# A two-layer transformer kernel: the last batch's tail reordered, second-layer heads one to a slot

## What is computed

```python
x = L0_attn_query
xn = _layernorm(x, axis=-1)
x = x + _L0_attn_ref(xn, ...) + _L0_ffn_ref(xn, ...)
xn = _layernorm(x, axis=-1)
x = x + _L1_attn_ref(xn, ...) + _L1_ffn_ref(xn, ...)
```

## Time and profile before

| | |
|---|---|
| median of 3 runs | 957.77 us (956.62 to 958.67) |
| the profiled execution | 958.63 us, span 956.8 us |
| TensorE (matmuls) busy | 830.6 us, 87% |
| VectorE busy | 742.3 us, 78% |
| ScalarE busy | 689.1 us, 72% |
| GpSimd busy | 471.4 us, 49% |
| TensorE clock granted, mean | 0.937 of full |

### The profile page before, as it was taken

The page is one execution under the profiler, slowest core; times in us unless marked ns, Lnnn a source line. Parts: engine busy times, 40 slices in busy tenths (PEclk is TensorE's granted clock), DMA queues, the critical chain, the costliest instruction groups (busy, mean ns, idle before and its releaser), DMA issues.

```text
span 956.8 us, 21194 instructions
## 1 busy us (share of the span) xinstructions
PE 830.6 (87%) x7120; PEld 609.9 (64%) x7120; DVE 742.3 (78%) x2028; ACT 689.1 (72%) x1973; POOL 471.4 (49%) x734
## 2 busy tenths in 40 slices
PE   3555538999899999999999999999999999996763
PEld 1123225687677777777777777777777777764541
DVE  6988855766768788887878787878787878875684
ACT  2654625656669778887888888788778878884673
POOL 1443332412326565665666555656565656566452
PEclk9675778999999999999999999999999999998896
DMA  9543412212243456554564555455556554544454
GB/s 331 196 148 110 133 52 82 52 34 43 48 103 75 90 93 140 102 83 108 123 105 78 115 116 111 77 124 102 107 80 143 89 101 89 123 98 93 114 107 102
DMA packets 283179, 100.97 MB, mean 106 GB/s; under 512 B 241344, under 2 KB 281024, under 8 KB 281920
## 3 DMA queue, kind: packets, MB, share of 16 engines
q1 hardware_dynamic: 280368, 97.27, 45.9%
q10 hardware_dynamic: 2704, 2.36, 0.7%
HBM read 30.38 MB, written 10.49 MB: 43 GB/s over the span
## 4 chain that ended last, share of the span: by engine, by line
PE 68%; DVE 9%; ACT 3%; issue 2%; DMA 1%; POOL 1%; SPq 0%; POOLq 0%; DVEq 0%; ACTq 0%
PE ps L666 42%; PE ps L716 9%; PE ps L816 4%; PE ps L799 4%; PE ps L692 3%; DVE arena L660 2%; PE ps L825 2%; PE ps L801 2%; PE ps L729 2%; DVE arena L999 1%; ACT arena L655 1%; DMA arena<-arena 1%; ACT arena L875 1%; DVE arena L659 1%; DVE nb L1006 1%
## 5 line engine op out<-in xcount | busy, mean ns | idle before, releaser
L660 DVE SCALAR_TENSOR_TENSOR arena<-ps,bqk,arena 128x256 bf16<-128x256 f32 x416 | 187.4, 479 | 63.3 <-ACT arena L655 61.8
L666 PE MATMUL ps<-arena,wqkv 128*128 128x256 bf16 x1728 | 215.2, 275 | 6.5 <-PEq L210 6.5
L655 ACT ACTIVATE arena<-ps,bqk 128x256 bf16<-128x256 f32 x416 | 177.9, 466 | 30.0 <-PE ps L666 20.8
L666 PEld LDWEIGHTS ps<-arena,wqkv 128*128 128x128 bf16 x1728 | 161.7, 98 | 48.1 <-issue 28.3
L1174 POOL TENSOR_SCALAR arena<-arena,rc 128x128 f32<-128x128 f32 (+1 forms) x256 | 106.3, 428 | 174.4 <-DVE rc L1022 174.4
L875 ACT ACTIVATE arena<-arena,nb 128x128 f32<-128x128 f32 (+1 forms) x256 | 114.3, 447 | 90.0 <-DVE nb L999 89.4
L1165 POOL TENSOR_TENSOR arena<-arena 128x512 bf16<-128x512 f32 x107 | 124.8, 1167 | 69.8 <-ACT arena L654 69.8
L1181 POOL TENSOR_SCALAR arena<-arena,rc 128x256 f32<-128x256 f32 x256 | 120.1, 483 | 75.7 <-DVE rc L1026 75.7
L654 ACT ACTIVATE arena<-arena 128x384 bf16<-128x384 f32 (+1 forms) x256 | 136.6, 572 | 18.7 <-POOL arena L1181 9.8
L875 ACT ACTIVATE arena<-ps,nb 128x256 f32<-128x256 f32 x256 | 118.6, 473 | 13.3 <-DVE nb L1006 10.8
L716 PE MATMUL ps<-wo,arena 128*128 128x256 bf16 x768 | 105.6, 274 | 10.5 <-DVE arena L660 9.8
(11 more groups left out here) (98 smaller groups left out, 1286.4 us busy)
## 6 DMA issues: line engine op xcount, KB each, us to landing
arena<-scratch_qk SPq DMA_DIRECT2D x96, 64.0 KB, 2.2
arena<-arena SPq DMA_TRANSPOSE x256, 2.7
scratch_qk<-arena SPq DMA_DIRECT2D x32, 128.0 KB, 1.9
arena<-in_x SPq DMA_DIRECT2D x4, 512.0 KB, 8.6
arena<-in_w_gating SPq DMA_DIRECT2D x2, 1024.0 KB, 6.7
arena<-in_w_q SPq DMA_DIRECT2D x2, 1024.0 KB, 8.6
scratch_xT<-arena ACTq DMA_DIRECT2D x8, 256.0 KB, 6.4
arena<-in_w_k SPq DMA_DIRECT2D x2, 1024.0 KB, 6.4
```

Of the source, the lines that this page charges most:

```text
L655: return nc.scalar.activation(out, in_, ACT.Identity, bias=bias)
L660: return nc.vector.scalar_tensor_tensor(out=out, in0=in_, scalar=bias, in1=hi, op0=ALU.add, op1=ALU.subtract)
L666: last = nc.tensor.matmul(out, lhsT, rhs, start=(n == 0), stop=(n == len(steps) - 1))
```

## The change

It touches the tables of slots and the order of steps from slot 131 on.

- `LATE` is 106, and the heads from there on have **one slot each**, 134 to 155, where they had two to a slot. The pipeline has ten more slots.
- The low part of these heads **alternates**: even heads on GpSimd, odd heads on VectorE (`low_on_pool`).
- In the last batch `x1_sum`, `variance`, `rstd_1` and `normalise` are in one slot, 131, ahead of that slot's maximum.
- The turn is in slot 132 and q/k/v in slot 133, one sooner. Their high and low parts come first in the slot on ScalarE and VectorE, and the q/k/v products first on TensorE.
- The hidden pieces and the down products are one slot sooner too (from slots 134 and 136), and the first steps of `up_gate` wait for x1T explicitly.

```diff
-        LATE = (B - 1) * H1 - 5
+        LATE = (B - 1) * H1 - 6
...
-            return start1(n // H1) + 12 + n % H1 if n < LATE else start1(LASTB) + 7 + (n - LATE) // 2
+            return start1(n // H1) + 12 + n % H1 if n < LATE else start1(LASTB) + 6 + n - LATE
...
-            return start1(b) + (7 + 2 * m if b < LASTB else 7 + m)
+            return start1(b) + (7 + 2 * m if b < LASTB else 6 + m)
...
-            return start1(b) + (6 if b < LASTB else 5)
+            return start1(b) + (6 if b < LASTB else 4)
...
+        def low_on_pool(n):
+            return n < LATE or n % 2 == 0
...
-        ln_in = by_slot(lambda b: start1(b) + 4, B)
+        ln_in = by_slot(lambda b: start1(b) + (4 if b < LASTB else 3), B)
...
                 upto(pe, v0_lo, min(s // 2 + 1, NG0 // 2))
+                pe.wait_ge(x1T_lo, b + 1)
...
             for s in range(SLOTS):
+                last = s >= NG0
+                if last:
+                    for n in pieces_in[s]:
+                        proj_qkv1(n)
                 if 0 <= s - 1 < NG0:
                     scores0(s - 1)
...
+                last = s >= NG0
+                if last:
+                    for b in turns_in[s]:
+                        x1T_low(b)
+                    for n in pieces_in[s]:
+                        qkv1_low(n)
                 if 0 <= s - 1 < NG0:
                     max_0(s - 1)
                 if 0 <= s - 4 < NG0:
                     o0_low(s - 4)
+                if last:
+                    for b in x1_in[s]:
+                        x1_sum(b)
                 for b in ln_in[s]:
                     variance(b)
+                    if last:
+                        normalise(b)
                 for n in heads_in[s]:
                     max_1(n)
...
                 for n in heads_in[s - 1]:
-                    if n >= LATE:
+                    if not low_on_pool(n):
                         p1_low(n)
```

More of the change, by code:

```diff
@@ L552, in hidden_slot @@
             b, m = divmod(n, KH)
-            return start1(b) + (7 + 2 * m if b < LASTB else 7 + m)
+            return start1(b) + (7 + 2 * m if b < LASTB else 6 + m)
         def down_slot(n):
             b, k = divmod(n, KH)
-            return start1(b) + (16 + k if b < LASTB else 9 + k)
+            return start1(b) + (16 + k if b < LASTB else 8 + k)
         def y_slot(b):
@@ L563, in piece_slot @@
             b, w = divmod(n, 3)
-            return start1(b) + ((7, 8, 11)[w] if b < LASTB else 6)
+            return start1(b) + ((7, 8, 11)[w] if b < LASTB else 5)
         def piece_bank(n):
@@ L645, in p1_split @@
         def p1_split(eng, n):
-            if n < LATE:
-                upto(eng, p1_lo, n + 1)
+            if low_on_pool(n):
+                upto(eng, p1_lo, sum(low_on_pool(z) for z in range(n + 1)))
             else:
-                upto(eng, p1_late, n - LATE + 1)
+                upto(eng, p1_late, sum(not low_on_pool(z) for z in range(n + 1)))
         def high(out, in_, bias=None):
@@ L859, in pe_program @@
                     transpose_x1(b)
-                for n in pieces_in[s]:
-                    proj_qkv1(n)
+                if not last:
+                    for n in pieces_in[s]:
+                        proj_qkv1(n)
                 if 0 <= s - 3 < NG0:
@@ L961, in act_program @@
             for s in range(SLOTS):
+                last = s >= NG0
+                if last:
+                    for b in turns_in[s]:
+                        x1T_high(b)
+                    for n in pieces_in[s]:
+                        qkv1_high(n)
                 if 0 <= s - 4 < NG0:
@@ L1145, in dve_program @@
                     rec_1(n)
-                for b in x1_in[s]:
-                    x1_sum(b)
+                if not last:
+                    for b in x1_in[s]:
+                        x1_sum(b)
                 if v_in(s) is not None:
@@ L1151, in dve_program @@
                     hidden(n)
[L1152 to L1157, removed]
+                if not last:
+                    for b in turns_in[s]:
+                        x1T_low(b)
+                    for n in pieces_in[s]:
+                        qkv1_low(n)
+                    for b in ln_in[s]:
+                        normalise(b)
                 for b in y_in[s]:
```

## The result

| | before | after |
|---|---|---|
| median of the runs | 957.77 us | **974.2 us** (970.64 to 976.07) |
| ratio | | **1.0161**, 95% interval 1.0144 to 1.0179 |
| profiled execution, span | 958.63, 956.8 us | 970.64, 968.8 us |
| VectorE busy, 905 to 935 us | 25.08 of 30 us | 16.82 of 30 us |

The ratio and its interval are those on record; the two medians of the table alone give 1.0172. The change makes the kernel slower, as forecast, but the time was missed: the forecast was 967.8 us for the median and 968.6 for the profiled execution, with a range of 962 to 974, and the median of 974.2 lies 0.2 us above that range. Four more executions of the same kernel (run 1) have a median of 972.87, inside it.

The account below looks back on a forecast made before the run. The prediction took VectorE's work and the engines' hand-offs, shared by two heads, as the bound. Start plus 3.2, heads 106 to 127 plus 7.6, tail minus 0.8 made plus 10.0 us: 967.8 us, range 962 to 974.

Parts of the forecast that it names:

- The ring of the earlier trace: Late heads: exponentials, reciprocal, norm, high part, next exponentials across three engines; some 2.85 us per head alone in a slot.
- The start, +3.2: Up to head 106's exponentials: sooner x1, but q/k/v's parts stand ahead of head 105; head 106 at 888.95, plus 3.2 us.
- Hidden slots, 26.0 us: Slots 134 to 141, one head and a hidden piece each: eight steps at 3.25 us, 26.0 us.
- Bare slots, 38.4 us: Slots 142 to 155, a head alone: 13 steps at 2.85 us plus 0.45 us on each of three, 38.4 us.
- Tail, -0.8: From head 127's exponentials to the end: an output's low part no longer stands ahead of its low part, minus 0.8 us.
- VectorE's work as the bound: Rival: VectorE's work sets the late heads' pace, so moving low parts off it gives 948 us; chance 0.06.
- No difference: Rival: slots are only an order, so the time stays within 0.2%, at 959.8 us; chance 0.05.
- TensorE slow in hidden slots: Rival: TensorE granted only 1.2 GHz from slot 134 on, 7.7 us more, 975.5 us; chance 0.10.
- VectorE and GpSimd in each other's way: Rival: GpSimd's low part meets the hidden piece's cast in four hidden slots, 4.5 us more, 972.3 us; chance 0.09.
- Low parts at nothing: Late heads: alternating low parts between GpSimd and VectorE isn't on the way to the next head, so costs nothing.

Follow-up runs that it names:

- Run 8: Run 7's kernel with VectorE's low parts of the bare slots one slot later, ahead of the reciprocal; 964.01 us, ratio 1.0061.
- run 5: The changed kernel with all low parts of the late heads on VectorE, still one head to a slot; 973.22 us, ratio 1.0164.
- run 10: The changed kernel with two heads to a slot, q's reads in slot 135, k's in 136, and all low parts on VectorE; 955.83 us, ratio 0.9976.
- Run 4: The changed kernel with SyncE's twelve reads of q and k spread three to a slot over slots 135 to 138; 968.0 us, ratio 1.0116.
- Run 6: The changed kernel with the attention products of the bare slots two slots later; 972.69 us, ratio 1.0157.
- run 2: The kernel before with only one edit, heads from LATE on one to a slot; 971.14 us, ratio 1.0141.
- Run 7: Run 6's kernel with, in bare slots, ScalarE's high part of the previous head behind the next head's exponentials, low parts moved back too; 967.66 us, ratio 1.0103.

## Why the prediction was right on the bound and missed the time

**The bound.** Right. The ring of the earlier trace rows set the pace of one head to a slot, and VectorE is 56% busy where under 60 was forecast. GpSimd's norm waits for the reciprocal, though not each time as forecast: from 917 to 955 us 9 times, while ScalarE's high part waits for the norm 13 times. Where it doesn't wait, a low part on GpSimd fills the time until the reciprocal is there (918.77 + 1.15 = 919.92, the reciprocal at 919.63 + 0.17). Run 8 shows the ring from the other side. The rule of the Trainium skill ("Perfetto Trace Analysis", Identifying the Most-Contended Engine) to optimise the busiest engine first would have given 948 us with one head to a slot; run 5 shows its step at no change, and run 10 shows the same step at 2.8 us with two heads to a slot, where VectorE is 75 to 80% busy.

**The start, +3.2.** Measured +2.5. The turn started at 875.25 us and q/k/v at 877.60, each 0.9 sooner than forecast, of which 0.74 is the earlier start of the last projection, a matter of chance. Head 105 came at 884.31, where 885.7 was forecast. One term inside was too small: the normalising took 1.56 us where 0.91 was taken, beside GpSimd's low part (last section).

**Hidden slots, 26.0 us.** Seven of eight steps are 3.17 us where 3.25 was taken, 0.6 less together. The eighth is 6.04. **This is the step that failed:** "SyncE issues these reads ahead of the transposes of heads 106 and 107, which has room: a high part asks for the transpose of three heads earlier". It had not. Twelve issues at 0.5 us are 6.0 us of SyncE's queue, and a transpose behind them belongs to an attention product only two slots later. The step was taken at 3.25 us and measured 6.04. The 0.5 us stands in the trace of before, in SyncE's queue:

```profile
893.73 5.74 SPq L1268 DMA_DIRECT2D arena<-scratch_qk  x12
```

I looked at how early the reads came, and not at how long they hold the queue. Run 4 took this wait away and 2.7 us with it.

**Bare slots, 38.4 us.** Measured 39.58, so 0.09 us a step too few. Four heads cost 2.81 + 2.80 + 3.36 + 3.25 = 12.2 us and not 11.85: behind an output two steps are longer, not one. Run 6 got 1.1 us of that back.

**Tail, -0.8.** Measured -0.75, and for the reason given: head 127's low part starts 2.95 us after its exponentials (958.23 and 955.28), where it started 3.69 after.

**Sum.** 2.8 for the reads, 1.2 in bare slots, less 0.7 at the start and 0.6 in hidden slots, are 2.7 us over the forecast in the end (12.7 against 10.0). The profiled execution took 970.64 where 968.6 was forecast; it began the last projection 0.74 us sooner than before. The median lies another 3.6 us higher, where I took it 0.86 below.

So of the 6.4 us between forecast and median, 2.0 stand in the trace and 4.4 in a second step that failed: "The median of the runs, 957.77, lies 0.86 lower". It took one profiled execution of the kernel before as the measure for another kernel, and one execution can't show that. Here the profiled execution was the fastest of four, as it was in runs 1 and 2. What makes the others slower is not shown. Up to 2.7 us can be TensorE's clock in slots 137 and 138, as in the profile of run 6, and 2.2 us lies ahead of the last projection in run 1 (870.21 against 868.00). How often that happens stays open, with two traces of this kernel.

**The rivals.** VectorE's work as the bound: refuted for one head to a slot (runs 2, 5, 8). No difference: refuted. TensorE slow in hidden slots: not in slots 134 to 141 as a whole, but the lower clock is seen in slots 137 and 138 of runs 6 and 8, behind the wait for the transpose, at a third of the price that was put on it. VectorE and GpSimd in each other's way: not at the casts, which took 0.29 us in the hidden slots of the timeline, but at other places (below).

**Low parts at nothing:** right for this change (run 5), wrong as a rule (run 10).

## What to carry to other kernels

Before spreading work over more slots of a software pipeline, count the round trips between engines that a slot holds: items that share a slot share the trip. When every engine is under 60% busy and the list of waits is a ring, change the order inside the slot (make what closes the ring come after what opens it) before moving work to another engine; here 2.2 us a head came from 3.04 that way. And count a burst of DMA issues as time on its queue: what stands behind it isn't issued until the burst is out. Three reads a slot left a wait of 0.28 us where twelve at once made one of 2.99.

## What the runs showed of the hardware

**Norms beside a low part.** GpSimd's two halves of a norm take 0.93 us with no low part beside them and 1.36 when VectorE's low part, a subtraction with two operands in SBUF, starts beside them. Run 7, GpSimd:

```profile
924.50 1.36 POOL L1219 TENSOR_SCALAR arena<-arena,rc 128x256 f32<-128x256 f32 x2 [0.51 <-DVE rc L1048]
927.47 0.93 POOL L1219 TENSOR_SCALAR arena<-arena,rc 128x256 f32<-128x256 f32 x2 [1.60 <-DVE rc L1048]
```

The low part that started at 924.76 on VectorE ran 0.76 us, and another at 929.56 ran 0.95, where 0.68 is what it takes elsewhere. Both sides lose. The kernel after has the same with other instructions: normalising x1 on VectorE, in two halves, takes 1.56 us beside GpSimd's low part of 1.16 (from 871.60 on). In the kernel before it took 0.91 beside a norm of GpSimd.

```profile
871.66 1.56 DVE L1110 TENSOR_SCALAR arena<-arena,mv,rs 128x256 f32<-128x256 f32 x2 [0.83 <-POOL rs L1225]
```

By the Trainium skill ("SBUF — State Buffer", on the shared port pair) one of the two engines holds the pair for a whole instruction and the other blocks. The rows agree: the norm started at 924.50, so its first half ends near 924.97; the low part started at 924.76 and ended at 925.52; and the second half ended at 925.86, so it began near 925.4, when the low part was about done. Where the low part began 0.06 us after the norm (929.56 and 929.50) it took 0.95. The normalising fits: its slowest half is 1.24 us, where the median of that line is 0.41, and the other half began at 872.8, when GpSimd's low part had ended (872.76). Which forms of instruction meet in this way no run here sorts out: this one has one tensor operand and two small ones, the low part two tensors.

**A wait can cost TensorE twice.** After 3 us without a product in slot 137 the next products ran at the full granted clock in the kernel after (up and gate 1.49 us) and at the lower of its two levels, 1.2 GHz, in run 6 (2.74 us), with the same instructions and a wait as long (2.99 and 3.06 us). So the same stall cost 2.9 us in one execution and 5.6 in the other. In the seven traces of one head to a slot in which this product waits 2.67 to 3.58 us, the full clock followed in five, the one with 3.58 us among them, and the lower level in two (runs 6 and 8, 3.06 and 3.05 us). So the length of the wait didn't decide it; what did is not shown.
